# Row maxima of two heads in one instruction, and the first pass of round 0 ahead of the scores

## What is computed

```python
def _attn(x, ctx, Wq, Wk, Wv, Wo, bo):
    ...
    sim = jnp.einsum('bihd,bjhd->bhij', q, k) * scale
    attn = jax.nn.softmax(sim, axis=-1)
    out = jnp.einsum('bhij,bjhd->bihd', attn, v).reshape(b, n, INNER)
    return out @ Wo + bo
...
x = _attn(h, h, Wq1, Wk1, Wv1, Wo1, bo1) + x
...
x = _attn(h, context, Wq2, Wk2, Wv2, Wo2, bo2) + x
...
x = a * jax.nn.gelu(gate, approximate=False) @ W2 + b2 + x
```

## Time and profile before

| | us |
|---|---|
| median of 3 runs (1997.73 to 1999.17) | 1997.93 |
| the profiled execution | 1998.15 |
| its span, first to last instruction | 1996.4 |
| PE busy (matmuls) | 1989.2 |
| DVE busy | 1391.5 |
| ACT busy | 1127.7 |
| POOL busy | 1490.1 |

### The profile page before, as it was taken

How to read it: one execution, slowest core, us unless ns; L and a number is a source line. 1 busy time by engine, 2 the same in 40 slices (tenths; PEclk the granted TensorE clock), 3 DMA queues, 4 the chain that set the end, 5 groups by cost and what they waited for, 6 DMA issues and landing times.

```text
span 1996.4 us, 32750 instructions
## 1 busy us (share of the span) xinstructions
PE 1989.2 (100%) x12568; PEld 1390.7 (70%) x12568; DVE 1391.5 (70%) x2766; ACT 1127.7 (56%) x1914; POOL 1490.1 (75%) x800
## 2 busy tenths in 40 slices
PE   9999999999999999999999999999999999999999
PEld 7655656666665656856656666665669999888888
DVE  6687687666867876587787566857867898744443
ACT  6565566555656665455666554656746776533332
POOL 3799899988989998899899889989887675200000
PEclk9999999999999999999999999999999999999999
DMA  8201000001000000010000001000030520000100
GB/s 286 75 32 38 6 7 17 18 16 48 17 12 6 17 6 27 19 46 6 7 22 7 27 1 53 7 27 1 22 106 15 154 67 1 1 22 31 34 12 32
DMA packets 48956, 67.19 MB, mean 34 GB/s; under 512 B 6176, under 2 KB 42144, under 8 KB 46752
## 3 DMA queue, kind: packets, MB, share of 16 engines
q1 hardware_dynamic: 48800, 65.10, 10.2%
HBM read 45.17 MB, written 19.92 MB: 33 GB/s over the span
## 4 chain that ended last, share of the span: by engine, by line
PE 99%; DVE 1%; issue 0%; POOL 0%; POOLq 0%
PE score L559 21%; PE score L542 18%; PE score L685 9%; PE score L546 6%; PE score L497 5%; PE attn_project L699 5%; PE attn_project L670 5%; PE first_score L523 5%; PE score L640 4%; PE attn_project L497 4%; PE score L509 3%; PE score L608 2%; PE attn_project L608 2%; PE attn_project L509 1%; PE first_score L654 1%; PE attn_project L523 1%
## 5 line engine op out<-in xcount | busy, mean ns | idle before, releaser
L1489 POOL TENSOR_TENSOR acc<-acc,pT 128x1024 f32<-128x1024 f32 x384 | 918.1, 2391 | 54.7 <-POOL acc L1489 1.8
L1233 ACT ACTIVATE pT<-score 128x1024 f32<-128x1024 f32 x512 | 525.4, 1027 | 137.8 <-PE score L546 89.5
L542 PE MATMUL score<-qk 64*128 64x512 f32 x3072 | 456.8, 399 | 0.4 <-ACT pT L1233 0.4
L559 PE MATMUL score<-pT,vT 128*64 128x512 f32 x1952 | 432.3, 595 | 0.0
L873 DVE TENSOR_REDUCE nmax<-first_score 128x1 f32<-128x512 f32 x512 | 347.8, 679 | 3.1 <-PE first_score L523 1.5
L873 DVE TENSOR_REDUCE nmax<-attn_project 128x1 f32<-128x512 f32 x512 | 347.0, 678 | 0.0
L542 PEld LDWEIGHTS score<-qk 64*128 64x128 f32 x3072 | 259.7, 185 | 114.5 <-ACT pT L1233 64.7
L559 PEld LDWEIGHTS score<-pT,vT 128*64 128x64 f32 x1952 | 134.7, 137 | 266.1 <-issue 243.9
L546 PE MATMUL score<-shift,pick 64*128 64x512 f32 x1024 | 205.8, 390 | 0.0
L523 PE MATMUL attn_project<-qk 64*128 64x512 f32 x512 | 203.0, 396 | 0.0
L523 PE MATMUL first_score<-qk 64*128 64x512 f32 x512 | 202.9, 396 | 0.0
(11 more groups left out here) (196 smaller groups left out, 3212.7 us busy)
## 6 DMA issues: line engine op xcount, KB each, us to landing
xres<-x_middle SPq DMA_DIRECT2D x10, 512.0 KB, 3.6
raw_qk<-in_L_xattn_Wq SPq DMA_DIRECT2D x32, 128.0 KB, 2.2
raw_qk<-in_L_xattn_Wk SPq DMA_DIRECT2D x32, 128.0 KB, 2.3
raw_v<-in_L_xattn_Wv SPq DMA_DIRECT2D x8, 512.0 KB, 4.2
keys_all<-keys SPq DMA_DIRECT2D x1, 4096.0 KB, 13.1
values_all<-values SPq DMA_DIRECT2D x1, 4096.0 KB, 12.4
out_x<-xres SPq DMA_DIRECT2D x7, 512.0 KB, 2.9
xres<-in_x SPq DMA_DIRECT2D x3, 1024.0 KB, 6.7
```

The source lines that it names most:

```text
L542: e.matmul(bank, qk[P % 2][r, 2 + h, keys], qk[P % 2][r, w, queries], start=(part == 0), stop=False)
L559: last = e.matmul(banks[bank][head * DH:(head + 1) * DH, :], vT[:, v_slot(D, jt), c0:c0 + DH], pT[:, jt, head, :], start=(jt == 0), stop=( ...
L1233: e.activation(pT[:, jt].rearrange("p h n -> p (h n)"), SC[R % 2][:, :], ACT.Exp).then_inc(s.exponential, 1)
L1489: e.tensor_tensor(total, total, pT[:, jt], ALU.add).then_inc(s.probs_added, 1)
```

## The change

1. The first passes of both heads with the same half now write one tile: half 0 writes T0 and T1, half 1 writes PV and PJ. `row_max` waits for both heads and is one instruction over the two banks, 128 x 2 from 128 x 1024. There are 512 of them in place of 1024, and `row_max`'s semaphore counts 1 for what was 2.
2. The first pass with jt = 0 is issued at the start of the stage, before round 0; the other seven stay behind their rounds.
3. Jobs of the slot move between banks: the first q/k projection from S1b to PV; tiles of v and output products from PV, S0b, S1a to S1b, S0b, S1a; the two turned halves of a layer norm from PV, T0 to S1b, S0b.

```diff
...
-        PASS_BANKS = (("T0", "T1"), ("PV", "PJ"))
+        PASS_BANKS = (("T0", "PV"), ("T1", "PJ"))
+        PASS_PAIRS = (FS, PX)
...
-        def passed(C, t, half, head):
+        def passed(C, t, half):
 
-            return 2 * TILES * C + 2 * (CHUNKS * t + half) + head + 1
+            return TILES * C + CHUNKS * t + half + 1
...
-            through = ("PV", "T0") if between and between[0][0] == "ln" else ("PV", "S0b", "S1a")
+            through = ("S1b", "S0b", "S1a")
             if 1 <= C < NC - 1:
                 jobs += [("sum", C - 1, "T1")]
             jobs += [(*job, through[i % len(through)]) for i, job in enumerate(between)]
             after = P + 1 + c
             if after < B * PAIRS:
-                jobs += [("qk", after, 1 - c, "S1b")]
+                jobs += [("qk", after, 1 - c, "PV")]
             if after < B * PAIRS:
                 jobs += [("qk", after, 3 - c, "PJ")]
...
-                free[bank] = ((s.row_max, passed(C, t, half, head)),)
+                free[bank] = ((s.row_max, passed(C, t, half)),)
...
             for C in range(NC):
+                if C + 1 < NC:
+                    for head in range(2):
+                        first_score(*next_part(C + 1, 0), head)
                 for jt in range(TILES):
...
-                    if C + 1 < NC:
+                    if C + 1 < NC and jt:
                         for head in range(2):
                             first_score(*next_part(C + 1, jt), head)
...
-            def row_max(C, t, half, head):
-                need.wait_ge(first_scored[head], TILES * C + CHUNKS * t + half + 1)
+            def row_max(C, t, half):
                 need.wait_ge(s.max_in, C)
-                e.tensor_reduce(nmax[:, head, t, half:half + 1], banks[PASS_BANKS[head][half]], AX.X, ALU.max,
+                for head in range(2):
+                    need.wait_ge(first_scored[head], passed(C, t, half))
+                e.tensor_reduce(nmax[:, :, t, half], PASS_PAIRS[half][:, :].rearrange("p (h n) -> p h n", h=2), AX.X, ALU.max,
                                 negate=True).then_inc(s.row_max, 1)
...
```

More of the change, by code:

```diff
@@ L868, in split_qk @@
                                        ALU.mult, ALU.subtract).then_inc(s.split_lo, 1)
-            def row_max(C, t, half, head):
-                need.wait_ge(first_scored[head], TILES * C + CHUNKS * t + half + 1)
+            def row_max(C, t, half):
                 need.wait_ge(s.max_in, C)
-                e.tensor_reduce(nmax[:, head, t, half:half + 1], banks[PASS_BANKS[head][half]], AX.X, ALU.max,
+                for head in range(2):
+                    need.wait_ge(first_scored[head], passed(C, t, half))
+                e.tensor_reduce(nmax[:, :, t, half], PASS_PAIRS[half][:, :].rearrange("p (h n) -> p h n", h=2), AX.X, ALU.max,
                                 negate=True).then_inc(s.row_max, 1)
             def gather_max(C):
-                need.wait_ge(s.row_max, passed(C, TPC - 1, CHUNKS - 1, 1))
+                need.wait_ge(s.row_max, passed(C, TPC - 1, CHUNKS - 1))
                 need.wait_ge(s.max_turned, C)
@@ L1026, in _ @@
             for i in range(TILES):
-                for head in range(2):
-                    row_max(*next_part(0, i), head)
+                row_max(*next_part(0, i))
             gather_max(0)
@@ L1037, in _ @@
                     for i in range(TILES):
-                        for head in range(2):
-                            row_max(*next_part(C + 1, i), head)
+                        row_max(*next_part(C + 1, i))
                     gather_max(C + 1)
```

## The result

The changed kernel takes 2016.4 us (median of 4 runs, 2015.15 to 2018.17), the kernel before 1998.05 (4 runs, 1997.73 to 1999.17). The ratio is 1.0092, 95% interval 1.0077 to 1.0106: slower by 18.4 us. The profiled execution of the changed kernel took 2017.45 us, its span 2015.7.

The account below looks back on a forecast made before the run. PE was taken as the bound, its loop of round 0, exponential and round 2 without slack. 12.8 + 4.1 + 1.8 - 0.4 = +18.3 us on the median 1997.93 gave 2016.2 us, range 2009 to 2021.

Parts of the forecast that it names:

- The lead: First pass ahead of round 0: round 2 waits for round 0's exponential, 0.23 us in each of 55 stages, +12.8 us.
- What would show it: Trace signs: round 2 starts 2.57 to 2.66 us into a stage, PE idles there, stages 0.23 longer, after norms 0.6.
- The paired reduction: One row-maxima instruction for two heads: lasts 1.22 us, repeats every 1.13, frees DVE of some 35 us; worth 0.
- The rival of a slow pair: Rival: a pair takes 1.36 us, DVE falls behind each round and first passes wait; 2029 us, chance 0.05.
- The banks after a norm: Seven stages after a layer norm: head 1 of round 0 waits for S0b; 0.59 us each, +4.1 us.
- The last stages: Stages 61 and 62: first passes and products wait for banks T0, T1 and PV; +1.8 us (0.5 to 2.5).
- Before the loop: Stage 0's eight passes: DVE's pairs at 1.13 us instead of 1.20 give back at most 0.4 us.
- The lead is hidden: Rival: round 2's weight load may come late without harm, so only the other terms stay; 2001.8 us, chance 0.06.
- The reductions pace the rounds: Rival: DVE's reductions set the length of rounds, which fall to 1.13 us; faster, 1984 us, chance 0.03.

Follow-up runs that it names:

- no_lead: The changed kernel with the first pass of round 0 put back behind its round, paired reductions and new banks kept: 2000.98 us, ratio 1.0015.
- lead_alone: The kernel before with only the first pass of round 0 moved ahead of it, single reductions and old banks kept: 2019.44 us, ratio 1.0108.
- short_exp: The changed kernel with round 0's exponential covering only 768 of 1024 columns in 50 stages: 2006.38 us, ratio 1.0043.
- long_exp: The kernel before with round 0's exponential in four pieces of 256 columns: 2007.55 us, ratio 1.0048.
- ln_banks: The changed kernel with the second turned half of a layer norm in S1a in place of S0b: 2012.32 us, ratio 1.0073.
- two_reductions: The changed kernel with row maxima taken by one instruction for each head again, banks, waits and first-pass order as changed: 2016.16 us, ratio 1.0090.

## Why the prediction was right, point by point

It said 2016.2 us, and 2016.4 came out. The terms for the stages were forecast at 12.8 + 4.1 + 1.8 = 18.7 us and measured 18.9. That the sum is close to 0.2 us is partly luck: the 0.4 forecast to come back before the loop did not, and the variation of the program's two ends, 0.5 us here, hides it.

- **The lead, +12.8 forecast.** Measured 54 x 0.236 + 0.23 = 13.0 in the 55 stages. The mechanism is shown from four sides: it goes with the lead (no_lead), comes with it alone (lead_alone), goes when the exponential is 0.2 shorter (short_exp), and appears without it when the exponential is 0.19 longer (long_exp). The last stage of the old kernel, had told the constant rightly: round 2 starts 1.54 us after the last step of round 0 there, and so it does in stage C = 34 of the changed kernel.
- **What would show it.** Round 2 at 2.58 us into the stage (2.57 to 2.66 forecast), stages longer by 0.23 and, after a norm, by nearly 0.6: as said. PE's idle of 0.1 in each stage is not in the profile, though: the first pass before it is shown until 827.14, so the wait of 0.16 beyond its step lies wholly beneath it.
- **The paired reduction, 0 forecast.** Right. A pair takes 1225 ns (forecast 1220), and ahead of the loop pairs follow each other at 1.14 where DVE is behind (38.39 less 37.25, forecast 1.13). The Trainium skill ("VectorE: DVE Perf Modes", section on the TRN2 errata) gives 120 cycles beside the elements for a read from PSUM; read as a spacing, an estimate of 1.19 us, it is not borne out by the 1.14. The rival of a slow pair is gone. One reading of the prediction was wrong, without weight for the time: DVE was to be freed of some 35 us, and the page has 5.6 less (1391.5 to 1385.9). In the loop the pairs can't follow each other at 1.13, since PE delivers one only with each round.
- **The banks after a norm, +4.1 forecast.** Measured 6 x 0.563 = 3.4, and C = 61 of the same size. ln_banks shows the cause. In stage C = 13 the load waits for the split that ends at 332.46, and the exponential is 2.01 us into the stage, where it is 1.50 in C = 34: the 0.51 of the forecast. But the prediction added the lead's 0.23 to the bank's own 0.36 (0.51 less the 0.15), and they do not add: without the lead these stages lose as much, 0.58 (no_lead). The total was right with the lead in place, the split was not. Timeline of the changed kernel:

```profile
331.74 0.50 PE L524 MATMUL first_score<-qk 64*128 64x512 f32 x2
331.77 0.69 DVE L838 TENSOR_TENSOR hT<-score,hT 128x512 fp32r<-128x512 f32 x1
...
332.51 0.53 PEld L543 LDWEIGHTS score<-qk 64*128 64x128 f32 x5 [0.48 <-DVE hT L838]
...
333.75 1.03 ACT L1236 ACTIVATE pT<-score 128x1024 f32<-128x1024 f32 x1 [1.30 <-PE score L547]
```

- **The last stages, +1.8 forecast.** Measured 1.38 - 0.56 + 1.45 - 0.24 = 2.0. Stage 62 begins with the wait for T0 (released by ACT's copy at 1454.79) and T1 (DVE until 1455.06), and ends with the wait for the last reduction: 1.81 us from the last first pass (1464.55) to the products, where 1.70 was forecast, since DVE is a little behind. The timeline of the changed kernel at the start of stage 62:

```profile
1454.20 0.59 ACT L1259 COPY oT<-first_score 128x512 f32<-128x512 f32 x1 [2.19 <-PE first_score L560]
1454.53 0.53 DVE L910 RECIPROCAL rsum<-first_score 64x16 f32<-64x16 f32 x2 [3.13 <-PE first_score L571]
...
1454.93 0.68 PE L524 MATMUL first_score<-qk 64*128 64x512 f32 x2 [0.44 <-ACT oT L1259]
```

and at the end of its rounds:

```profile
1464.55 0.40 PE L524 MATMUL attn_project<-qk 64*128 64x512 f32 x2
1465.08 1.23 DVE L878 TENSOR_REDUCE nmax<-attn_project 128x2 f32<-128x1024 f32 x1
...
1466.36 1.08 PE L560 MATMUL attn_project<-pT,vT 128*64 128x512 f32 x4 [1.42 <-DVE nmax L878]
```

- **Before the loop, -0.4 forecast.** This step failed; from the first to the eighth pass of stage 0 it is 8.49 us, and it was 8.50. DVE, which was busy throughout, now starts a pair 1.22 after the one before (38.39 to 39.61) where it could after 1.14, but ACT has four copies out of PSUM for every two passes, which I had not looked at. DVE and ACT there, in the changed kernel's timeline:

```profile
37.25 1.23 DVE L878 TENSOR_REDUCE nmax<-attn_project 128x2 f32<-128x1024 f32 x1
38.39 1.22 DVE L878 TENSOR_REDUCE nmax<-first_score 128x2 f32<-128x1024 f32 x1
39.61 1.23 DVE L878 TENSOR_REDUCE nmax<-attn_project 128x2 f32<-128x1024 f32 x1
...
36.92 2.17 ACT L1209 COPY values<-score 128x512 f32<-128x512 f32 x4 [0.25 <-PE score L485]
39.31 2.17 ACT L1209 COPY values<-score 128x512 f32<-128x512 f32 x4 [0.22 <-PE score L485]
```

Four copies take 2.17, and the next four start 2.39 later, the time of two passes. PE's weight loads for the products between the passes wait for these copies, before (first row) and after alike:

```profile
PEld score L484 <- ACT values L1206: 1.0, 3, 0.3
...
PEld score L485 <- ACT values L1209: 1.0, 3, 0.3
```

I had taken a full DVE for the only bound there. That PE and ACT set the pace between them is read from these rows; no run tested it.

- **The rivals.** "The lead is hidden" fell with long_exp: the 0.1 us by which the load stands ahead of the matmul is no room, since the stage grew by all of the 0.19. "The reductions pace the rounds" fell with two_reductions and no_lead: with either spacing of DVE an ordinary stage is the same within 0.003.

The 18.4 us between the medians are 0.5 less than the stages' 18.9. The rest is of the size by which the ends of the program vary; what it is made of stays open.

## What to carry to other kernels

Work that stands between two uses of a double buffer is what hides the consumer; count the producer's steps from the last write of one use to the first of the next, and compare them with the consumer's latency, before moving one of them. A wait of a weight load beneath a running matmul is no loss by itself, but it can mean that there is no slack left, as here, and then every step moved away costs its full length, once in each stage. Taking time off an engine that nobody waits for gives nothing, and a bank that is freed last should go to the work that wants it last.

## What the runs showed of the chip

**The ends of the program vary with the clock.** In the last stage PE waits for the folded sums (L570, 2.8 us in the kernel before). In the profiled execution of the kernel before, the granted clock around the end of that wait was 0.66 on average over ten microseconds, that is 6.8 of them at 1.2 GHz; in that of the changed kernel, where the wait was 2.8 us too, it was 0.83, 3.4 of ten; and in that of no_lead, where the wait was 1.3 us, it did not fall. Busy time by stretch (columns as in the earlier trace rows; the number behind POOL's is the granted clock), of the kernel before:

```profile
1460.00:1470.00 10.00, 7.33 (x28) 3.98 (x30) 5.44 (x6) 3.06 (x4) 9.84 (x5) 0.66 0.15 37
```

of the changed kernel:

```profile
1480.00:1490.00 10.00, 7.23 (x38) 3.78 (x36) 6.07 (x6) 3.67 (x4) 9.71 (x5) 0.83 0.11 32
```

and of no_lead:

```profile
1466.00:1476.00 10.00, 8.71 (x52) 3.86 (x50) 4.71 (x6) 3.70 (x4) 9.71 (x6) 1.00 0.44 90
```

That is most of what the column "from C = 63 on" holds: -1.3 with the fall halved, -3.5 without it. In two_reductions (a wait of 2.2 us) and ln_banks (2.8) it did not fall either, so the length of that wait alone doesn't decide it. What decides whether the clock falls, the runs don't tell. A change of 1 or 2 us is thus seen by the stages' lengths in a trace long before it is seen in the times. **Ahead of the loop** the kernels are nearly the same, and yet the loop began up to 1.8 us apart; part of it is PE's wait for weights that DMA brings (0.6 us at L434 in the changed kernel, none such among the matmul waits of the kernel before). Where the rest comes from stays open.

**Four ACT instructions on 256 columns cost 0.27 us each** in a row, from start to start, and one on 1024 columns lasts 1.03: splitting the exponential cost 0.06 us for each cut, though each short instruction lasts 0.39 us by itself.
